# Cross attention: the reciprocal rows are loaded back by SyncE instead of ScalarE, with one store semaphore per slot

## What is computed

```python
q = (text_hidden @ Wq).reshape(B, T_text, N_HEADS, HEAD_DIM).transpose(0, 2, 1, 3)
...
scores = jnp.einsum('bhtd,bhsd->bhts', q, k) / scale
...
attn = jax.nn.softmax(scores, axis=-1)
...
out = jnp.einsum('bhts,bhsd->bhtd', attn, v)
...
return out @ Wo
```

## Time and profile before

| | |
|---|---|
| median of 3 runs | 1905.4 us (1905.21 to 1907.29) |
| the profiled execution | 1908.66 us, of which the span is 1906.7 us |
| TensorE clock granted, mean over the span | 0.982 |
| busy | PE 1828.8 us (96%), DVE 1276.3 (67%), ACT 929.8 (49%), POOL 623.2 (33%) |
| DMA queue q1 (SP) | 60067 packets, 112.74 MB |
| DMA queue q10 (ACT) | 38912 packets, 14.80 MB |

### The profile page before, as it was taken

How to read it: one execution, slowest core, us unless ns; L and a number is a source line. 1 busy time by engine, 2 the same in 40 slices (tenths; PEclk the granted TensorE clock), 3 DMA queues, 4 the chain that set the end, 5 groups by cost and what they waited for, 6 DMA issues and landing times. The chain is left out here.

```text
span 1906.7 us, 29800 instructions
## 1 busy us (share of the span) xinstructions
PE 1828.8 (96%) x10628; PEld 1632.1 (86%) x10628; DVE 1276.3 (67%) x3469; ACT 929.8 (49%) x1646; POOL 623.2 (33%) x360
## 2 busy tenths in 40 slices
PE   6999789999999999999999999999999958999998
PEld 6888679898989989998998989989998956888886
DVE  4655467778787787777778777787877726445544
ACT  4333355556565555656556565565656522322221
POOL 1120244533344353334434334353334019000010
PEclk9999899999999999999999999999999978999999
DMA  4233662424323242332334333243331024010000
GB/s 177 68 111 103 191 97 60 79 66 82 65 57 61 78 89 42 83 61 57 71 71 89 46 76 61 67 86 54 84 62 27 18 68 123 1 30 10 10 20 10
DMA packets 99113, 129.28 MB, mean 68 GB/s; under 512 B 36239, under 2 KB 79921, under 8 KB 98833
## 3 DMA queue, kind: packets, MB, share of 16 engines
q1 hardware_dynamic: 60067, 112.74, 25.1%
q10 hardware_dynamic: 38912, 14.80, 4.2%
HBM read 107.22 MB, written 20.30 MB: 67 GB/s over the span
## 5 line engine op out<-in xcount | busy, mean ns | idle before, releaser
L789 ACT CAST b_pT_hi<-b_turn 125x512 fp32r<-125x512 f32 (+1 forms) x768 | 406.3, 530 | 546.8 <-PE b_turn L729 543.2
L883 DVE TENSOR_TENSOR b_pT_lo<-b_turn,b_pT_hi 125x512 fp32r<-125x512 f32 (+1 forms) x768 | 478.1, 623 | 268.7 <-ACT b_pT_hi L789 262.5
L869 DVE CUSTOM_DVE_ANT_0 b_p<-b_score,b_mask_add 128x500 f32<-128x500 f32 x672 | 451.8, 673 | 55.6 <-PE b_turn L729 23.8
L729 PEld LDWEIGHTS b_turn<-b_ident,b_p 128*125 128x125 f32 x2688 | 410.0, 186 | 57.6 <-issue 1.1
L729 PE MATMUL b_turn<-b_ident,b_p 128*125 128x128 f32 x2688 | 418.5, 272 | 0.7 <-ACT b_p L795 0.7
L795 ACT ACTIVATE b_p<-b_p,b_shift 128x1500 f32<-128x1500 f32 x224 | 347.4, 1551 | 16.6 <-DMA rden_store<-b_rden 8.5
L746 PE MATMUL b_out<-b_pT_hi,b_c_hi 125*128 125x512 f32 (+1 forms) x768 | 346.6, 451 | 8.0 <-DVE b_pT_lo L883 8.0
L748 PE MATMUL b_out<-b_pT_hi,b_c_lo 125*128 125x512 f32 (+1 forms) x768 | 281.2, 366 | 0.0
L747 PE MATMUL b_out<-b_pT_lo,b_c_hi 125*128 125x512 f32 (+1 forms) x768 | 281.2, 366 | 0.0
L1010 POOL TENSOR_TENSOR b_oT_lo<-b_oT,b_oT_hi 128x896 fp32r<-128x896 f32 x32 | 67.8, 2118 | 642.8 <-ACT b_oT_hi L817 642.8
L715 PE MATMUL b_score<-b_cT_hi,b_q_hi 128*128 128x500 f32 x672 | 264.2, 393 | 9.5 <-DVE b_cT_lo L956 9.5
(11 more groups left out here) (175 smaller groups left out, 2858.5 us busy)
## 6 DMA issues: line engine op xcount, KB each, us to landing
cT_in<-in_ctxT SPq DMA_DIRECT2D x32, 750.0 KB, 11.7
b_c_in<-in_ctx SPq DMA_DIRECT2D x32, 750.0 KB
q_store<-a_fold_in_or_q_stage SPq DMA_DIRECT2D x16, 896.0 KB, 4.1
q_in<-q_store SPq DMA_DIRECT2D x32, 448.0 KB, 8.1
b_rden_all<-rden_store ACTq DMA_DIRECT2D x32, 256.0 KB, 4.1
b_rden_all<-rden_store ACTq DMA_DIRECT2D x32, 192.0 KB, 4.6
b_mask_in<-in_mask SPq DMA_DIRECT2D x32, 187.5 KB, 10.7
c_w_in<-in_hidden SPq DMA_DIRECT2D x16, 256.0 KB, 3.1
```

Source lines behind the costliest of these rows:

```text
L729: mm = pe.transpose(turn_bank[n % 3][0:CK, u * 128:(u + 1) * 128], p[slot % 2][:, u, c * CK:(c + 1) * CK], ident[:])
L789: act.copy(pT_hi[:, n % 3, 0:w], turn_bank[n % 3][0:CK, 0:w]).then_inc(hi_done, 1)
L869: dve.tensor_tensor_reduce(out=p[slot % 2][:, u, keys], in0=score_bank[j][:, 0:FW], in1=mask_add[:, b, keys], scale=1.0, scalar=-3.0e38, o ...
L883: dve.tensor_tensor(pT_lo[:, n % 3, 0:w], turn_bank[n % 3][0:CK, 0:w], pT_hi[:, n % 3, 0:w].bitcast(F32), ALU.subtract).then_inc(lo_done, 1)
```

## The change

SP issues the load of every rden row instead of ACT. The store stays on ACT where it was, but it counts in a semaphore of its own for each slot, so that SP can wait for 16 x (i + 1). In SP's program the load of (i - 2, 3) comes behind the scores loads of (i, b = 0), that of (i - 1, 0) behind the values load of b = 0, that of (i - 1, 1) behind the residual, and that of (i - 1, 2) behind the values load of b = 1. For pair 1 the first of these is left out, and the last five are written out behind the loop.

```diff
-        rden_done, rden_stored = sem("rden_done"), sem("rden_stored")
+        rden_done = sem("rden_done")
+        rden_stored = [sem(f"rden_stored{k}") for k in range(SLOTS)]
...
-        RDEN_AT, STORE_AT, LOAD_AT = 3, 4, 11
+        RDEN_AT, STORE_AT = 3, 4
...
+            def load_rden(i, slot):
+
+                w = 128 * units(slot)
+                sp.wait_ge(rden_stored[slot], 16 * (i + 1))
+                sp.dma_start(rden_all[:, slot % 2, 0:w],
+                              D["rden"][bass.ds(i, 1), slot, 0:w].rearrange("a n -> (a n)").partition_broadcast(
+                                  128)).then_inc(rden_loaded[slot % 2], 16)
+
             def loads(i, first=False):
                 load_q(i, 0)
                 load_scores(i, 0)
+                if not first:
+                    load_rden(i - 2, 3)
                 load_values(i, 0)
+                load_rden(i - 1, 0)
                 load_q(i, 1)
                 load_scores(i, 1)
                 if not first:
                     store(i - 2)
                 residual(i - 1)
+                load_rden(i - 1, 1)
                 load_values(i, 1)
+                load_rden(i - 1, 2)
 
             loads(1, first=True)
             with sp.Fori(2, NPAIR) as i:
                 loads(i)
+            load_rden(NPAIR - 2, 3)
+            load_rden(NPAIR - 1, 0)
             store(NPAIR - 2)
             residual(NPAIR - 1)
+            for slot in range(1, SLOTS):
+                load_rden(NPAIR - 1, slot)
             store(NPAIR - 1)
...
-                              rden[:, slot % 2, 0:u], allow_slow_non_contiguous=True).then_inc(rden_stored, 16)
-
-            def load_rden(i, slot):
-
-                w = 128 * units(slot)
-                act.wait_ge(rden_stored, 16 * (SLOTS * i + slot + 1))
-                act.dma_start(rden_all[:, slot % 2, 0:w],
-                              D["rden"][bass.ds(i, 1), slot, 0:w].rearrange("a n -> (a n)").partition_broadcast(
-                                  128)).then_inc(rden_loaded[slot % 2], 16)
+                              rden[:, slot % 2, 0:u], allow_slow_non_contiguous=True).then_inc(rden_stored[slot], 16)
...
-                if n % CH == LOAD_AT and (at := lagging_slot(i, n, 1, first, last)):
-                    load_rden(*at)
```

## The result

The changed kernel takes 1917.53 us in the median of 5 runs (1914.57 to 1920.55) against 1906.18 us (1905.21 to 1907.29) for the kernel before, run beside it: a ratio of 1.0058, with a 95% interval of 1.0046 to 1.0070. It is slower by 11.35 us. In a later set of runs the same kernel gave 1913.05 against 1905.38 us, 1.0033 (1.0021 to 1.0045). So the loss is real, and its size, between 0.2 and 0.7%, differs more from one set of runs to the next than either interval says. One of the 11 executions of the kernel of experiment 2 (first set) took 3674 us, for a reason that is not known; no ratio uses it.

What follows compares the result with a forecast made beforehand. PE was taken to bound mid-phase, so only pair 0's stalls count: PE 9.8 us later plus 2.3 us at low clock, + 12.1 us, all else 0. That gives 1920.8 us profiled, 1917.5 us as median; range 1906.5 to 1923.

Steps and rivals of the forecast that it cites:

- the likeliest case: Pair 0: the store of (0, 1) holds the values load and the row behind it; 1914.5 to 1920.7 us, chance 0.56.
- No gain in the middle of the phase: Pair 7: PE is busy 82.10 of 82.10 us, so taking load and wait off ACT is worth 0.
- ACT's stall goes, and the store of (0, 1) comes at 254.2: Pair 0: ACT goes on at 245.35 and stores (0, 1) 8.85 us later, 1.4 us ahead of the values load.
- The values load at 255.65, the row behind it: Pair 0, SP: load time stays, row of (0, 0) issued at 256.0; another load time would show the prediction wrong.
- The store holds the values load: Pair 0: the values load crawls while the store of (0, 1) is out, up to 11.9 us, until 266.1.
- The row lands at 275.0: Row of (0, 0): 266.1 plus 8.9 us, as for (7, 2) in pair 7; bounds 272.0 and 278.2.
- PE restarts 2.0 us behind DVE and pays 2.3 us for the clock: Pair 0, step 31: PE weighs at 277.0 instead of 267.16, + 9.8 us, and loses 2.3 us at low clock.
- The sum: Whole kernel: 12.1 + 0 + 0 us, 1920.8 on the profiled execution, 1917.5 us as the runs' median.
- The other slots: Later rows: slots 0, 1 and 3 hidden; slot 2 comes 1 us later, DVE waits 0.6 us, cost 0.
- the row lands like a lone load: Pair 0, faster rival: row not held behind the values load, lands at 259.2; 1898 to 1899.4 us, chance 0.10.
- the price of today's stall: Pair 0, kernel before: PE stands 6.07 us and loses 2.3 us at low clock, 8.4 us, once.
- The prediction's sentence on the fixed cost of a DMA: Skill page: about 2.0 us per DMA; by it the store of (0, 1) ends before the values load starts, 1907.4 us.

Runs made afterwards that it cites:

- experiment 2: Kernel before with only the load of (0, 0) moved to SP behind the values load, other 63 rows on ACT: 1912.77 us, 1.0031; in a second set 1914.88, 1.0044.
- experiment 3: Changed kernel with the store of (0, 1) in step 31 instead of 28: 1908.85 us, 1.0007 to the kernel before.
- Experiment 4: Changed kernel with each row stored as 128 packets of 16 or 12 bytes instead of 512 or 384 of 4: 1902.31 us, 0.9981 to the kernel before.
- experiment 1: Changed kernel with SP issuing the row of (0, 0) ahead of the values load: 1900.19 us, 0.9961 to the kernel before; again 1900.09, 0.9972.

## Why the prediction held, and where it was off

The time forecast was 1917.5 us, and the way there was that of the likeliest case. That the first set's median is 1917.53 is luck: two terms of the sum were wrong in opposite directions, and the second set gave 1913.05. Its steps:

- *No gain in the middle of the phase.* Right: with the waits of ACT gone, no pair is shorter; the scalings of pairs 1 to 14 keep their distance.
- *ACT's stall goes, and the store of (0, 1) comes at 254.2.* It came at 254.18.
- *The values load at 255.65, the row behind it.* The load went out at 254.27, 1.4 us sooner, which the prediction itself had named as a sign of being wrong: POOL was held by the DMA of the values before, and that landed sooner. This is more than chance. In all eleven traces with 4-byte stores in which ACT does not stand for the store of (0, 0), the values load goes out 17.9 to 19.3 us behind that store, in the trace of before 20.6. Why, no run tells. The order against the store of (0, 1), 0.1 us, was a near thing, and the three traces of experiment 2 with the order turned round show that the loss does not hang on it: they lose 4.1 or 4.2 us in pair 0 and this one 8.3.
- *The store holds the values load.* Right by the stretches at 51 and 244 GB/s, and shown by experiment 3. Experiment 4 shows what makes the store long.
- *The row lands at 275.0.* It landed at 271.3, under the lower bound of 272.0, and both terms were mis-sized. The store of (0, 1) was to be out for 11.9 us at most, until 266.1; it was out for 16.9, until 271.1 (the 18.5 us of pair 0 had been a warning). And the row was to land 8.9 us behind the store; it landed 0.2 us behind it. I let the values load begin when the store was through. The DMA engines moved 147 GB/s for 3 us before the crawl, 51 GB/s during it, and 244 GB/s after 266, while the store was still out. The pattern from pair 7 did not fit, since there the load came 10 us behind the store and met only its end.
- *PE restarts 2.0 us behind DVE and pays 2.3 us for the clock.* 273.46 - 271.39 = 2.07, and 2.1.
- *The sum.* By the trace it is + 9.0 us of span, not + 12.1: 8.2 in pair 0, 0.4 given back at the last scaling, and 1.2 behind it, in the rest of phase_b and phase_c, which I had at 0. The median's + 11.35 lies nearer to the forecast than the mechanism was, and the second set's + 7.7 farther: the forecast was some 3 us too high for this trace and 8 for the three in which the store went out last, and the first set of runs hid it.
- *The other slots.* Right. The row of slot 2 made DVE wait 0.8 us once, at (3, 2), less often than the 0.6 us in each pair that I had charged, and PE had the spare time for it. SP's queue was hardly a worse place than ACT's: rows behind a values load land after 8.6 to 11.1 us in pairs 1 to 14, where those of slot 2, issued beside one on ACT's queue, took 8.8 to 10.4 before.
- *The rivals.* That the row lands like a lone load needs it ahead of the values load: experiment 1 makes that version. It also checks the 8.4 us that the prediction had named as the price of today's stall. In the four traces with the row first, the scalings from (0, 1) to (15, 2) stand 8.5 us ahead of those of before, each taken from its own store of (0, 0). The medians of the two sets show 6.5 and 6.0 us.
- *The page.* The prediction's sentence on the fixed cost of a DMA (the Trainium skill, page "DMA: Bandwidth & Descriptors", section "Anatomy of one DMA") says more than its source: that section is on DMAs issued by GpSimd, and these are ACT's. By its figure the store would be over at 256.2, 0.6 us behind the issue of the values load and not before it. Nothing in the sum hangs on this.

## What to carry to other kernels

A load for which an engine waits does not belong behind a bulk load of the same queue; look at the first turn of the pipeline apart, since in the steady state here some 16 us between the values load and the use of the row hid what cost 4 to 8 us in pair 0. Taking a wait off one engine also moves up everything that this engine issues later, and here a tiny store that came 8.5 us sooner met a load that it had missed before. A few hundred 4-byte writes to HBM are a long transfer whatever their bytes; count packets, not bytes.

## What the runs showed of the hardware

A store of 1.5 or 2 KB in 384 or 512 packets of 4 bytes lands 8.3 us after its issue at the least and 8.9 in the median; the first two of the changed kernel, issued within 1.2 us of a values load, took 18.7 and 16.9 us. In 128 packets of 12 or 16 bytes it takes 2.2 us in the median. While the first kind is out, there are stretches of 8 us in which the loads move 26 or 51 GB/s (pair 0) with the DMA engines over 90% busy, and 199 to 244 GB/s right after them. A load of 750 KB issued 2.5 us behind such a store takes 10.9 to 11.9 us, and 4.3 to 5.2 behind one in fewer packets; one issued up to 1 us ahead of it can be held too (experiment 2). Why the loads crawl, whether at the memory or in the engines, no run here tells.
